# Counting a graph's edges by tiles on one core: longer counted runs with a slot range for each tile, 896 nodes in nine slot blocks, and four tiles' row masks in one compare

## The reference

```python
S = layernorm(x)[src]
for r in (0, 1):                       # two dense layers a relation
    msgs = where(rel == r, relu(relu(S @ W_rel[r].T + b[r]) @ W_rel[r].T + b[r]), msgs)
agg = segment_sum(msgs, dst, num_segments=3125)
gates = agg @ W_ih.T + b_ih + b_hh     # i, f, g, o; no recurrent part
c = sigmoid(i) * tanh(g); hn = sigmoid(o) * tanh(c)
x = x + relu(relu(hn @ W1.T + b1) @ W2.T + b2) @ W3.T + b3
# then, with n = layernorm(x): the 1561 nodes (int(0.5 * 3125) - 1) with the highest
# score wr . n keep t = score * (gelu(n @ w1 + fb1) @ w2 + fb2), the others t = 0
x = x + t + n
```

## Time and profile before

| | |
|---|---|
| runs, median (lowest to highest) | 799.16 us (797.22 to 802.53) |
| the profiled execution's span | 796.5 us |
| PE busy | 703.9 us, 88% |
| VectorE busy | 437.6 us, 55% |
| ScalarE busy | 243.2 us, 31% |
| GpSimd busy | 417.8 us, 52% |
| mean granted PE clock | 0.954 |
| gathers: count, issue to landing | 400, 2.8 us |

### The profile page before, as it was taken

The page is one execution under the profiler, slowest core; times in us unless marked ns, Lnnn a source line. Parts: engine busy times, 40 slices in busy tenths (PEclk is TensorE's granted clock), DMA queues, the critical chain, the costliest instruction groups (busy, mean ns, idle before and its releaser), DMA issues.

```text
span 796.5 us, 9071 instructions
## 1 busy us (share of the span) xinstructions
PE 703.9 (88%) x2919; PEld 428.7 (54%) x2919; DVE 437.6 (55%) x1566; ACT 243.2 (31%) x418; POOL 417.8 (52%) x773
## 2 busy tenths in 40 slices
PE   2989994769799999889995799999999999699986
PEld 1676683225445555445652356566656556267655
DVE  6849779997988877660321504316026316114375
ACT  1343441121333333344031242332333133131701
POOL 6000004676767766776667677747327677762000
PEclk9999996589999999999997799999999999889999
DMA  9210213323333323333543333323113333331004
GB/s 273 73 58 12 96 63 104 91 86 93 96 90 87 93 74 93 102 87 96 191 133 92 90 105 90 100 66 93 47 46 93 93 93 92 102 92 45 1 1 161
DMA packets 39368, 71.67 MB, mean 90 GB/s; under 512 B 8448, under 2 KB 25873, under 8 KB 39313
## 3 DMA queue, kind: packets, MB, share of 16 engines
q0 software_dynamic: 19200, 52.45, 23.0%
q1 hardware_dynamic: 19296, 17.77, 7.0%
q10 hardware_dynamic: 816, 0.79, 0.3%
HBM read 61.23 MB, written 9.75 MB: 89 GB/s over the span
## 4 chain that ended last, share of the span: by engine, by line
PE 62%; DVE 14%; POOL 12%; issue 6%; DMA 3%; ACT 2%; SPq 0%; DVEq 0%; POOLq 0%
PE BIG L1150 19%; POOL ring L941 12%; PE SM L1233 10%; PE AG L1336 6%; PE SM L1317 6%; PE BIG L1109 6%; DVE oh_row L1651 4%; DVE oh_key L1641 3%; PE SM L1120 3%; DMA ring<-message_table,rowT 3%; PE AG L1120 3%; PE BIG L1187 2%; PE BIG L1304 2%; PE BIG L1090 2%; PE SM L1208 2%
## 5 line engine op out<-in xcount | busy, mean ns | idle before, releaser
L941 POOL DMA_INDIRECT ring<-message_table,rowT x400 | 396.2, 991 | 267.6 <-DMA message_table<-late 115.7
L1336 PE MATMUL AG<-ring,onehot 128*128 128x512 f16 x400 | 104.7, 394 | 23.2 <-DMA ring<-message_table,rowT 22.6
L1233 PE MATMUL SM<-half_b,late 128*128 128x256 f32 x400 | 94.0, 382 | 0.9 <-ACT late L1060 0.6
L1233 PEld LDWEIGHTS SM<-half_b,late 128*128 128x128 f32 x400 | 74.4, 190 | 18.4 <-issue 5.7
L1336 PEld LDWEIGHTS AG<-ring,onehot 128*128 128x128 f16 x400 | 44.3, 116 | 70.6 <-DMA ring<-message_table,rowT 21.8
L1150 PE MATMUL BIG<-fT,half_a 128*128 128x512 f32 (+1 forms) x192 | 81.8, 581 | 0.0
L1651 DVE TENSOR_SCALAR oh_row<-iota,lists 128x128 f16<-128x128 f16 x393 | 76.0, 270 | 5.9 <-PE BIG L1304 5.8
L1304 PE MATMUL BIG<-oh_key,oh_row 128*128 128x500 f16 (+8 forms) x225 | 61.3, 361 | 19.4 <-DVE oh_row L1651 18.1
L1641 DVE TENSOR_SCALAR oh_key<-iota,lists 128x500 f16<-128x500 f16 (+8 forms) x225 | 64.1, 334 | 19.2 <-PE BIG L1304 18.9
L1150 PE MATMUL BIG<-half_b,half_a 128*128 128x512 f32 (+2 forms) x200 | 73.0, 521 | 0.5 <-ACT half_b L1030 0.5
L1553 DVE TENSOR_TENSOR late<-late 128x1024 f32<-128x1024 f32 (+2 forms) x7 | 7.8, 1111 | 115.1 <-ACT late L1037 115.1
(11 more groups left out here) (197 smaller groups left out, 827.9 us busy)
## 6 DMA issues: line engine op xcount, KB each, us to landing
ring<-message_table,rowT POOLq DMA_INDIRECT x400, 2.8
message_table<-late SPq DMA_DIRECT2D x10, 512.0 KB, 3.5
out<-X SPq DMA_DIRECT2D x24, 128.0 KB
X<-in_x SPq DMA_DIRECT2D x4, 512.0 KB, 6.5
half_a<-in_f SPq DMA_DIRECT2D x1, 1024.0 KB, 5.1
half_b<-in_f SPq DMA_DIRECT2D x1, 1024.0 KB, 10.9
message_table<-late SPq DMA_DIRECT2D x2, 384.0 KB, 2.9
half_a<-in_w_ih_t SPq DMA_DIRECT2D x1, 768.0 KB, 4.5
```

Of the source, the lines that this page charges most:

```text
L941: nc.gpsimd.indirect_dma_start(ring[:, to * W:(to + 1) * W], None, table, bass.IndirectOffsetOnAxis(ap=rowT[:, t:t + 1], axis=0)).then_inc ...
L1233: last = nc.tensor.matmul(bank, hidden_of(s)[:, c, j * P:(j + 1) * P], F2[:, c, :], start=(c == 0), stop=(c == HC - 1))
L1336: mm = nc.tensor.matmul(AG[w % 2][:, :], hot[:, :, i], ring[:, to:to + W], start=(c == FIRST_OF[w] and i == lo), stop=(c == LAST_OF[w] and ...
```

## The change

It alters how the counting is divided, and what lies around it.

- HOT goes from 6 to 7 (896 nodes counted, TH = 424 tiles, COLD = 413: 369 tiles are gathered and not 400), NK from 10 to 9.
- A counted run has up to 32 tiles and up to 128 slots, and each tile has a slot range of its own in it (`offsets`), at most 10 wide. There are 47 runs; 15 of them lie below tile 212 and 32 from there on, and they are taken in turn (`riffled`). A run is cut into slot parts of at most 10 (`cut`, 138 in all), each with its own bank; a tile that lies in two or three parts issues two or three matmuls (`HALVES`).
- A quad's row masks are one `tensor_tensor` compare of 512 columns; the weights for PE then lie with a stride of four.
- The products of a block are cut into 25 pieces and not 12, and start as soon as the block's parts are evicted; planned times in `schedule` follow the width.
- Choosing: masks for 32-node grains, in both supers 0 and 1; the separate step "fifth" goes.
- GpSimd's bounds are set tile by tile, 698 memsets with a semaphore of their own. `make_windows` goes run by run. The weights W_ih are loaded after the last product (block 8 lies in `half_a`, where they go), before after the last but one.

```diff
-    HOT = 6
+    HOT = 7
-    KR, MORE_KEYS = 9, 7
+    KR, MORE_KEYS = 8, 7
-    NK = 10
+    NK = 9
...
-    TH = end_tile(HOT - 1)
+    TH = 4 * round(end_tile(HOT - 1) / 4)
...
     def windows():
-        best = {TH: (0.0, 0, 0)}
-        for t in range(TH - 1, -1, -1):
+        best = {TH: (0.0, 0, 0, [])}
+        for t in range(TH - 4, -1, -4):
             ways = []
-            for m in range(1, min(16, TH - t) + 1):
-                k = slots_for(t, m)
-                if k <= WIDE:
-                    ways.append((best[t + m][0] + k * (0.084 + 0.0209 * m) + 0.3, m, k))
+            for c in range(t, min(TH, t + 16)):
+                made = [offsets(c, i) for i in range(t - c, 0)]
+                for e in range(c, min(TH, t + 32)):
+                    made = made + [offsets(c, e - c)]
+                    if max(b - a for a, b in made) > WIDE:
+                        break
...
+    WINS = riffled(widened(windows()))
...
+    PARTS = [part for j in range(NWIN) for part in cut(j)]
+    HALVES = [[(p, max(lo, x), min(hi, y)) for p, (lo, hi) in enumerate(PARTS) if x < hi and y > lo] for _, x, y in TILES]
...
+    def bank_wait(p):
+        n = FIRST_IN[p]
+        return n - 1 if n % 2 == 0 and n and (p < 4 or DONE[p - 4] < n - 1) else n
...
-        PIECES = 12
+        PIECES = 25
...
         def hot_steps():
...
+            whole = [DONE[last_part(k)] + 3 for k in range(NK)] + [TH]
+            for n in range(TH):
+                made.append(("tile", n))
                 for k in range(NK):
...
+                    if whole[k] == n:
+                        made += due
+                        due = [("dense", (k, i)) for i in range(PIECES)]
...
-            sp.wait_ge(sm_full, at[("sm", "dense", NK - 2)] + 1)
+            sp.wait_ge(sm_full, at[("sm", "dense", (NK - 1) // 2 * 2)] + 1)
             sp.dma_start(WI, w_ih_t.rearrange("(c p) n -> p c n", p=P)).then_inc(late_in[0], 16)
...
-            for t, made in ((low_t, LOWS), (high_t, HIGHS), (span_t, SPANS)):
+            for t, made in ((low_t, LOWS), (high_t, HIGHS), (width_t, WIDTHS), (tile_low, OFFSETS)):
                 for lo, hi, v in made:
-                    nc.gpsimd.memset(t[:, lo:hi], float(v)).then_inc(consts, 1)
+                    nc.gpsimd.memset(t[:, lo:hi], float(v)).then_inc(bounds_set, 1)
...
+                due = [p for p in range(len(PARTS)) if bank_wait(p) == n]
+                if due:
+                    pe.wait_ge(big_free, at[("big", "window", due[-1])] - 3)
+                rows = oh_row[:, (n // 4 % RR) * 4 * P:(n // 4 % RR + 1) * 4 * P].rearrange("p (n t) -> p n t", t=4)
+                for p, lo, hi in HALVES[n]:
+                    at_slot = PARTS[p][0]
+                    mm = nc.tensor.matmul(BIG[at[("big", "window", p)] % 4][:, (lo - at_slot) * A:(hi - at_slot) * A],
+                                          rows[:, :, n % 4], key_slot(n)[:, (lo - first) * A:(hi - first) * A],
+                                          start=(n == FIRST_IN[p]), stop=(n == LAST_IN[p]), skip_group_check=True)
...
             def make_windows():
+                dve.wait_ge(bounds_set, N_BOUNDS)
                 dve.wait_ge(big_free, at[("big", "spread", 3)] + 1)
...
+                for j, (t, c, nodes) in enumerate(WINS):
+                    first, k, m = min(a for a, _ in nodes), slots_of(nodes), len(nodes)
+                    nc.vector.tensor_scalar(slot_row[:, SLOT0[j]:SLOT0[j] + k], iota16[:, 0:k], tmin_b[:, c:c + 1], float(first),
+                                            ALU.add, ALU.add)
+                    last = nc.vector.tensor_scalar(tile_low[:, t:t + m], tile_low[:, t:t + m], tmin_b[:, c:c + 1], None, ALU.add)
...
-                nc.vector.tensor_scalar(minus_row, keys_i[:, 0:TH], -1.0, None, ALU.mult)
+                for i in range(4):
+                    nc.vector.tensor_scalar(row16[:, :].rearrange("p (q t) -> p t q", t=4)[:, i, :],
+                                            keys_i[:, 0:TH].rearrange("p (q t) -> p t q", t=4)[:, i, :], 4.0, float(i),
+                                            ALU.mult, ALU.add)
...
             def rows(q):
                 if q >= RR:
                     dve.wait_ge(counted, ticked(4 * (q - RR) + 3))
-                for i in range(min(4, TH - 4 * q)):
-                    to = (q % RR) * 4 * P + i * P
-                    last = nc.vector.tensor_scalar(oh_row[:, to:to + P], iota16[:, 0:P], minus_row[:, 4 * q + i:4 * q + i + 1], 0.0,
-                                                   ALU.add, ALU.is_equal)
-                last.then_inc(rows_made, 1)
+                t, to = TILES[4 * q][0], (q % RR) * 4 * P
+                nc.vector.tensor_tensor(oh_row[:, to:to + 4 * P].rearrange("p (n t) -> p n t", t=4),
+                                        row16[:, t:t + 4].unsqueeze(1).broadcast_to([P, P, 4]),
+                                        iota16[:, 0:4 * P].rearrange("p (n t) -> p n t", t=4), ALU.is_equal).then_inc(rows_made, 1)
```

More of the change, by code:

```diff
@@ L127, in build @@
[L127 to L144 removed]
+            _, e, c, nodes = best[t]
@@ new lines, in windows, with slots_of, widened @@
+            made.append([t, c, nodes])
+            t = e
+        return made
+    def slots_of(nodes):
+        return max(b for _, b in nodes) - min(a for a, _ in nodes)
+    def widened(made):
+        spare = NK * P - sum(slots_of(nodes) for _, _, nodes in made)
+        assert spare >= 0
+        while spare:
+            before = spare
+            for _, _, nodes in made:
+                a, b = nodes[-1]
+                if spare and b - a < WIDE and b == max(z for _, z in nodes) and slots_of(nodes) < P:
+                    nodes[-1] = (a, b + 1)
+                    spare -= 1
+            assert spare < before
+        return made
@@ new lines, in riffled @@
+    def riffled(made):
+        ways = []
+        for x in range(1, len(made)):
+            order, low, high, ahead, worst = [], 0, x, 0, 0
+            while low < x or high < len(made):
+                if high < len(made) and (low == x or ahead < 0):
+                    order.append(high)
+                    high += 1
+                else:
+                    order.append(low)
+                    low += 1
+                ahead += slots_of(made[order[-1]][2]) * TH - len(made[order[-1]][2]) * NK * P
+                worst = max(worst, abs(ahead))
+            ways.append((worst, order))
+        return [made[j] for j in min(ways)[1]]
@@ new lines, in build @@
+    WINS = riffled(widened(windows()))
+    NWIN = len(WINS)
+    SLOT0 = [sum(slots_of(nodes) for _, _, nodes in WINS[:j]) for j in range(NWIN)]
+    TILES = []
+    for j, (t, c, nodes) in enumerate(WINS):
+        base = SLOT0[j] - min(a for a, _ in nodes)
+        TILES += [(t + i, base + a, base + b) for i, (a, b) in enumerate(nodes)]
+    OFFSET = {t + i: a for t, _, nodes in WINS for i, (a, _) in enumerate(nodes)}
+    WIDTH = {t: hi - lo for t, lo, hi in TILES}
+    assert len(TILES) == TH and all(TILES[n][0] % 4 == n % 4 for n in range(TH))
@@ new lines, in cut @@
+    def cut(j):
+        lo = SLOT0[j]
+        hi = lo + slots_of(WINS[j][2])
+        mine = [x for x in TILES if x[0] in range(WINS[j][0], WINS[j][0] + len(WINS[j][2]))]
+        best = {hi: (0.0, hi)}
+        for a in range(hi - 1, lo - 1, -1):
+            best[a] = min((best[z][0] + 0.35 + 0.05 * sum(x < z < y for _, x, y in mine), z)
+                          for z in range(a + 1, min(hi, a + WIDE) + 1))
+        made = []
+        while lo < hi:
+            made.append((lo, best[lo][1]))
+            lo = best[lo][1]
+        return made
@@ L406, in build @@
         rs = sb("rs", [P, NB])
-        wcol = sb("wcol", [P, NB])
+        wcol, mw, above = [keyT[:, i * NB:(i + 1) * NB] for i in range(3)]
         tmm = sb("tmm", [P, 2, TC])
@@ L456, in build @@
         consts = sem("consts")
+        bounds_set = sem("bounds_set")
         ident_ready = sem("ident_ready")
@@ L707, in other_orders @@
                         vector.append((end, 3, ("choose", 0)))
-                    j = WIN_OF[s]
-                    if WINS[j][0] + WINS[j][1] == s + 1:
-                        scalar.append((end, 2, ("evict", j)))
+                    scalar.extend((end, 2, ("evict", p)) for p in range(len(PARTS)) if DONE[p] == s)
                 elif kind == "dense":
@@ L1183, in phase @@
                         nc.tensor.matmul(b[:, 0:n], zeros16[:, :], iota16[:, 0:n], start=True, stop=False, skip_group_check=True)
[L1184 to L1188 removed]
+                        for i, (part, pick_of, lo, hi) in enumerate(parts):
+                            last = nc.tensor.matmul(b[:, lo:hi], part[:, c * P:(c + 1) * P], pick_of, start=False,
+                                                    stop=(i == len(parts) - 1), skip_group_check=True)
                         last.then_inc(big_full, 1)
```

354 lines of the change are left out of this document (153 added, 201 removed).

## The result

The changed kernel takes 778.45 us (median; 774.97 to 778.94) where the kernel before takes 799.12 on the same chip (797.22 to 802.53). The ratio is 0.9731, with a 95% interval of 0.9696 to 0.9767: 2.7% faster. The forecast was 759, within 745 to 780. The direction holds and the time lies inside the range, at its upper end: of a gain of 40 us only 21 came. Some executions of a program are slower than the rest, and every ratio here, with its interval, is taken from the fast ones alone, while a median counts all of a kernel's runs.

The account below looks back on a forecast made before the run. Masks on VectorE bound the second stretch and PE's work most of the rest, with no engine full throughout. 796.5 + 6.6 - 31.4 - 18.4 + 3 = 756.3 us span, 2.7 more for the median: 759, range 745 to 780.

Parts of the forecast that it names:

- Bounds on GpSimd: Table stage: 698 memsets for 111 end at about 42 us, before VectorE asks at 59.5; cost nothing.
- Rival 1: Counting after the first product: weight loads bound the split matmuls, +12 us, total 771; chance 0.12.
- rival 2: Row masks on VectorE: the one compare runs at an element a cycle, total 767; chance 0.10.
- window tables: Table stage on VectorE: 94 small instructions at 0.138 us take 13.0 us, +6.6, all passed on to gathers and counting.
- Rival 3: Table stage: window tables cost only what they do now, or the stall is absorbed; 753 to 755 us; chance 0.12.
- Before the first product: Masks of the first counted tiles on VectorE, which sets the pace: 22 us against 53.4, so -31.4.
- From the first product on: PE's stretch up to choosing: 171.5 us of work plus idle time, 194 against 212.4, so -18.4.
- The cheaper masks are worth nothing here: After the first product: VectorE needs 0.3 us a tile where PE needs 0.49, so faster masks gain nothing.
- Rival 4: Counting: 138 PSUM bank hand-overs stall PE waiting for ScalarE, costing 80 us, total 839; chance 0.04.
- Rival 5: Third stretch: idle time grows by what the masks gave, so nothing is gained, 790 to 806 us; chance 0.04.
- The rest: From choosing to the end: PE's work the same within 2 us, more gathered tiles left to visit, +3 us.
- second road: Check from GpSimd alone: gathers, pauses and full-ring waits end at 687 us, plus 73.8 behind them, 761.

Follow-up runs that it names:

- without the stall: Changed kernel with GpSimd waiting at every eighth memset and VectorE's table work cut in three: 754.92 us, 0.9453 of the kernel before.
- 907 chips: Two chips where the kernel before takes 907 and 910 us and TensorE stands still 32 to 61 us without a recorded cause in the program.

## Why the prediction was right, and where it wasn't

**The step that failed** is the first: "Bounds on GpSimd ... Cost nothing, with 17 us of cover." The cover was right by the waits: VectorE goes on to the bounds at 79.35, and they are set at 32.89, sooner than the 42 given. But a wait by semaphore is not the only way in which one engine holds another. The stream holds VectorE's tensor_scalar by running, and this costs 22.8 us in the changed kernel (9.47 + 13.89 less the usual 0.17 + 0.41). The kernel before paid 4.3 us of it already. The row was in the trace, 26 times longer than the same instruction later (0.17 us for four columns). The Trainium skill, "SBUF — State Buffer", section "Who interferes with whom", says that VectorE and GpSimd share a pair of ports, that tensor_scalar can enter a mode that needs it, that an instruction with one input outside of such modes doesn't need it, and that whoever comes second blocks for the whole instruction. The trace agrees as to which instructions are held: tensor_scalar is, bn_stats and bn_aggr are not. By that page's "whole instruction" VectorE would wait for one memset, 0.1 us. Here it is held until the 297 have ended and then until the other 401 (31 + 370) have. By the profile's starts the second one even begins before the memsets go on (19.15 and 19.25) and is held all the same. The measurement decides.

That the time lies inside the range all the same is luck. The upper part of the range was made for rivals 1 and 2, and neither came true; the stall fills that room with a cost that no rival had.

**The table stage else.** The window tables were put at 13.0 us and take 13.0 (79.35 to 92.32, 94 at 0.138 us). Against the kernel before, the layernorm ahead of them is 19.8 us late and the one behind them 26.7, so 6.9 us come in between, where 6.6 were forecast. Rival 3 (no dearer than now) is out. The chain "ScalarE evicts the slot nodes, a first-layer matmul waits" is there: 7.0 us, where the kernel before has no such wait. Behind that the prediction put nothing, but the lateness grows on, to 29.2 us at the first counted tile and 30.1 at the first gather, 0.5 of it by the four row conversions (3.82 us for the keys, 3.35 before).

With the stall gone the first gather is at 135.6 to 136.2, and the forecast was 135.2. This agreement is in part luck. The forecast was counted from a kernel that has a stall of its own, and some of that still shows at the fourth layernorm (first row the kernel before, second the one with gaps and fewer pauses). These 3.2 us stand against the 3.2 to 3.4 that come in behind the window tables and that the prediction put at nothing.

```profile
53.57 1.38 DVE L1408 TENSOR_SCALAR agg_ring<-X,mv,rs 128x256 f32<-128x256 f32 x4
```

```profile
50.41 1.38 DVE L1458 TENSOR_SCALAR agg_ring<-X,mv,rs 128x256 f32<-128x256 f32 x4
```

**Before the first product**: 20.2 us, 22 forecast. What follows a row compare starts 0.335 us after it (median of the 95 behind which VectorE didn't wait), as given, so rival 2 is out.

**From the first product on** the work was right and the idle time wrong. By columns 171.6 us of matmuls, forecast 171.5; the stretch is 183.3, and 176.8 without the stall, not 194. Idle are 11.7 and 5.2 us, where the prediction kept 20.5 of the 23.6 and added 2. Taken as the distance of two starts less the columns at 0.42 ns, 12.3 us of the idle time stood ahead of counting matmuls in the kernel before and 8.3 ahead of gathered tiles; now 1.5 and 7.5, and without the stall 1.5 and 1.3. PE's waits between the first product and choosing, in the kernel before:

```profile
PE AG L1336 <- DMA ring<-message_table,rowT: 6.1, 7, 1.4
PE BIG L1304 <- DVE oh_row L1651: 5.8, 7, 1.6
PE BIG L1164 <- issue: 1.0, 1, 1.0
PE BIG L1304 <- ACT half_b L1014: 1.0, 2, 0.6
PE BIG L1304 <- ACT half_a L1017: 0.6, 1, 0.6
PE SM L1317 <- ACT half_b L1017: 0.5, 2, 0.3
```

and after, again all there are:

```profile
PE AG L1384 <- DMA ring<-message_table,rowT: 6.5, 1, 6.5
PE SM L1365 <- ACT half_a L1087: 0.7, 1, 0.7
PE SM L1365 <- ACT half_a L1090: 0.4, 2, 0.2
```

"The cheaper masks are worth nothing here" was an argument from means. By the means VectorE needs 0.3 us a tile and PE 0.49, but the masks come in lumps of a quad, and PE did wait for them. Whether the one compare or the smoother order of low and high runs took these waits away isn't shown: the run that could tell (one compare alone) came to chips with stalls of their own.

**Rival 1**, weight loads that bound the split matmuls, is out. Between the first product and choosing, the median distance from a counting matmul to the matmul behind it is 28 ns at 50 columns (45 of them), 44 at 100 (56), 65 at 150 (72) and 107 at 250 (70): a little above their columns (21, 42, 62, 104), far from the 105 of a load. By 0.42 ns a column the 572 are 53 us, and 68 if none took less than 105 ns; the prediction's 54 and 69 are one too high each, which changes nothing. The 81 ns that the Trainium skill, "TensorE: Matmul & The Clock Gate", Back-to-back issue gap, gives for 128 columns in a stream of loads and matmuls don't show here either, where 150 columns come at 65 with weights that do change. **Rival 4**, the banks, is out too: the counting waits no more for ScalarE in that stretch. **Rival 5** is out as it was worded, but part of its idea came true further on.

**The rest** is 9.9 us longer than forecast, 416.7, and 15.5 longer without the stall (422.3, just beyond the 420 that the prediction set itself as a mark). It is the same sum read from the other end. PE reached the choosing earlier than forecast, the gathers didn't end earlier, and so PE waits for them there: over the whole run 32.0 us without the stall, 22.6 in the kernel before. The prediction's second road, from GpSimd alone, says that: 687 for the last gather at a start of 135.2; measured 679.9 at a start of 135.8. From the first gather on, the gathers and the work behind them take 616.9 us, and the prediction had 621.1. So without the stall the total would have been right to 4 us, and the errors of -17 and +15 in its two parts cancel not by luck but because the gathers bound the end, at least in part: of 16 us that fewer pauses should have brought by that, 9 came.

## What to carry to other kernels

Before small instructions are added on GpSimd in a place where it is idle, look at what VectorE runs in that place, not only at who waits for the result. A row that is many times longer than its twin later in the same trace can be a stall even where no wait is recorded, and what it ends with hints at whose; a run with that work added and one with it broken up show it. A long stream on GpSimd beside VectorE's tensor_scalar should have gaps in it. And where two streams run side by side to the end (here PE and the gathers), work out the end from the slower one, and take gains on the other as worth only what its own waits leave.

## What the runs showed of the hardware

GpSimd's memsets follow each other at 33 to 50 ns (402 in 13.30 us, 297 in 11.46, the 111 of the kernel before in 5.55), and while they do a VectorE tensor_scalar doesn't get through. Two sizes were seen, 4 and 256 fp32 columns: 4.48, 9.47, 9.74 and 10.08 us for an instruction of 0.17, 13.4 and 13.9 for one of 0.41. It gets through at the stream's end or in a gap of 0.5 to 0.6 us. A wait of GpSimd for its own last memset at every eighth lets it through, in 0.17 to 0.50 us (eight profiles). These waits stretch the memsets themselves from 25.7 us to 36.4. Why GpSimd has the one gap isn't known; it comes behind 297 memsets in the changed kernel and behind 296 (111 + 185) in the kernel before with 587 more.

On the 907 chips PE and the other engines stand still now and then for 1 to 11 us without a cause in the program's records. What that is stays open.
